# Attention output transposed by DMA planes instead of TensorE, in a linear-attention and soft-tree layer

## What is computed

```python
xn = layernorm(x)
Q, K = elu(xn @ Wq + bq) + 1, elu(xn @ Wk + bk) + 1   # 16 heads of 64
V = xn @ Wv + bv
KV_t = KV_{t-1} + k_t v_t^T ; Ks_t = Ks_{t-1} + k_t   # causal, per head
attn = (q_t KV_t) / (q_t . Ks_t + 1e-6)               # 16 heads side by side: 1024 features
tree = leaf_probs(sigmoid(xn @ Wt.T @ routers.T)) @ leaf_values @ Wout.T + bout   # 256 leaves
out = x + attn @ Wo + bo + tree
```

## Time and profile before

| | us |
|---|---|
| median of 3 runs | 1233.66 |
| range of the runs | 1233.03 to 1235.53 |
| the profiled execution, its own time | 1235.54 |
| its span, first to last instruction | 1233.8 |

### The profile page before, as it was taken

How to read it: one execution, slowest core, us unless ns; L and a number is a source line. 1 busy time by engine, 2 the same in 40 slices (tenths; PEclk the granted TensorE clock), 3 DMA queues, 4 the chain that set the end, 5 groups by cost and what they waited for, 6 DMA issues and landing times.

```text
span 1233.8 us, 48282 instructions
## 1 busy us (share of the span) xinstructions
PE 1202.1 (97%) x21669; PEld 1052.3 (85%) x21669; DVE 811.4 (66%) x2186; ACT 551.7 (45%) x881; POOL 675.5 (55%) x842
## 2 busy tenths in 40 slices
PE   5899999999999999999999999999999999999987
PEld 4789889898988989889898988989889898988967
DVE  4774876757667574875758667574866758667462
ACT  3553552535445253552535445253552535445251
POOL 3475556455554665556455554655556465554550
PEclk9999999999999999999999999999999999999998
DMA  6121211212123121222213122121222213122120
GB/s 230 20 53 36 57 34 45 54 36 54 36 46 53 37 54 36 57 34 45 54 36 54 36 46 53 36 54 36 55 36 45 53 36 54 36 45 36 37 36 19
DMA packets 154654, 58.94 MB, mean 48 GB/s; under 512 B 134081, under 2 KB 152784, under 8 KB 154448
## 3 DMA queue, kind: packets, MB, share of 16 engines
q1 hardware_dynamic: 154448, 55.86, 21.8%
HBM read 14.43 MB, written 8.39 MB: 18 GB/s over the span
## 4 chain that ended last, share of the span: by engine, by line
PE 95%; DVE 2%; ACT 1%; POOL 1%; DMA 1%; issue 1%; SPq 0%; POOLq 0%; DVEq 0%
PE s_pair L705 26%; PE w_pair L705 22%; PE o_pair L717 9%; PE s_pair L717 9%; PE o_pair L814 6%; PE s_pair L778 5%; PE o_pair L828 5%; PE kv_pair L789 5%; PE w_pair L758 5%; PE w_pair L740 2%; DMA ffn_tok<-in_L_ffn_Wout_w_dram 1%; ACT ex L455 0%; ACT ex L458 0%; PE o_pair L705 0%; DVE wk L250 0%
## 5 line engine op out<-in xcount | busy, mean ns | idle before, releaser
L353 POOL TENSOR_SCALAR_AFFINE_SELECT aT<-aT 64x512 f32<-64x512 f32 x256 | 167.7, 655 | 366.0 <-ACT aT L482 357.1
L482 ACT ACTIVATE aT<-s_pair 128x512 f32<-128x512 f32 x128 | 76.4, 597 | 337.6 <-PE s_pair L778 337.6
L705 PE MATMUL w_pair<-xnT,wk 128*128 128x512 f32 x768 | 212.3, 412 | 4.1 <-ACT k_tok L468 2.2
L705 PE MATMUL s_pair<-xnT,wq 128*128 128x512 f32 x756 | 200.9, 401 | 1.4 <-POOL aT L353 1.1
L632 DVE TENSOR_TENSOR snaps<-kv_pair,snaps 128x65 f32<-128x65 f32 x768 | 173.3, 226 | 26.5
L404 POOL COPY k_tok<-k_turned 128x1024 uint16<-128x1024 uint16 x126 | 171.4, 1361 | 29.6 <-POOL aT L353 22.6
L396 POOL COPY k_planes<-kT 128x1024 uint16<-128x1024 uint16 x126 | 131.2, 1041 | 95.1 <-POOL k_tok L404 58.2
L455 ACT ACTIVATE ex<-w_pair,neg_bias 128x512 f32<-128x512 f32 x130 | 89.6, 689 | 189.5 <-PE w_pair L705 189.5
L705 PE MATMUL s_pair<-wv,xnT 128*128 128x512 f32 x648 | 168.5, 394 | 0.1
L458 ACT ACTIVATE ex<-ex 128x512 f32<-128x512 f32 x256 | 161.9, 633 | 8.1
L705 PEld LDWEIGHTS w_pair<-xnT,wk 128*128 128x128 f32 x768 | 134.4, 188 | 36.2 <-ACT k_tok L468 2.7
(11 more groups left out here) (107 smaller groups left out, 1972.1 us busy)
## 6 DMA issues: line engine op xcount, KB each, us to landing
x_in<-in_L_attn_x_dram SPq DMA_DIRECT2D x16, 512.0 KB, 5.1
out_dram<-y_buf SPq DMA_DIRECT2D x32, 256.0 KB, 2.1
k_turned<-k_planes SPq DMA_TRANSPOSE x126, 3.1
stage<-in_L_attn_Wv_dram SPq DMA_DIRECT2D x2, 512.0 KB, 8.0
stage<-in_L_attn_Wk_dram SPq DMA_DIRECT2D x2, 512.0 KB, 9.6
stage<-in_L_attn_Wq_dram SPq DMA_DIRECT2D x2, 512.0 KB, 10.9
stage<-in_L_attn_Wo_dram SPq DMA_DIRECT2D x2, 512.0 KB, 9.4
bv_all<-in_L_attn_bv_dram SPq DMA_DIRECT2D x1, 512.0 KB, 8.6
```

The lines of the kernel that those rows point to most:

```text
L353: pool.affine_select(out=part, in_=part, compare_op=ALU.is_ge, fill=0.0, base=0, pattern=[[0, 2 * CH], [1, D]], channel_multiplier=-1).the ...
L482: act.activation(aT[:, n % 2].rearrange("p h c q -> p h (c q)"), s_pair[:, :, 0:CH * D], ACT.Copy).then_inc(s_copied, 1)
L705: last = pe.matmul(dst, l, r, start=i == 0, stop=i == len(steps) - 1)
```

## The change

For the units n >= 3 with p < 7 (`by_dma`, 109 of 128) the oT fill and what read it are gone. Their outputs are turned as the keys are: POOL copies the 16-bit halves of `o_tok` into two planes (`take_output_apart`, behind the mask), SP issues a transposing DMA ahead of that of the keys, and in the next unit ACT interleaves the two turned planes into a float32 tile (`put_output_together`, a 128 x 1024 copy of 16-bit elements in SBUF, behind the exponential of K and ahead of the head's work). ACT takes the high part from that tile behind the exponential of Q (`high_of_turned`), DVE the low part at the end of the unit (`low_of_turned`, both inputs in SBUF); at p = 7 both stand ahead of the high and low part of the remaining oT.

The head now fills bank S1 and the tail W1. DVE does `norm(n)` ahead of `carry(n+1)`. PE's waits stand elsewhere: at single matmuls, for the values at the outer products, for each output bank at its first use, and y waits for the low parts of tile t = 0 and t = 6 (`o_low`). Odd tiles of a block are kept with their halves swapped; for this each load of x is three DMAs instead of one, and each half store of a block three instead of one. The number of matmuls for everything else is the same.

```diff
+def by_dma(n):
+    return n % PAIRS < PAIRS - 1 and n >= 3
@@ unit_fills
-    fills += [(name, W1) for name in head]
+    fills += [(name, S1) for name in head]
...
-    fills += [(name, S1) for name in tail]
-    fills.append((("oT", p, g), W1))
+    fills += [(name, W1) for name in tail]
     if p == PAIRS - 1:
-        fills += [(("y", 0, g), O1), (("y", 1, g), S1)]
+        fills += [(("oT", p, g), W1), (("y", 0, g), O1), (("y", 1, g), S1)]
+    elif not by_dma(n):
+        fills.append((("oT", p, g), S1))
@@ SP
+            def load_block(g):
+                dst, src, done = x_in[:, g % 2], x_rows[g], x_loaded[g % 2]
+                sp.dma_start(dst[:, 0::2], src[:, 0::2]).then_inc(done, 16)
+                sp.dma_start(dst[0:D, 1::2], src[D:P, 1::2]).then_inc(done, 16)
+                sp.dma_start(dst[D:P, 1::2], src[0:D, 1::2]).then_inc(done, 16)
+            def turn_output(n):
+                g, p = divmod(n, PAIRS)
+                sp.wait_ge(o_apart, units_by_dma(n))
...
+                if n >= 5:
+                    sp.wait_ge(o_whole, units_by_dma(n) - 2)
+                sp.dma_start_transpose(o_turned(p), o_planes.rearrange("p s n -> p (s n)")).then_inc(o_turned_in, 16)
@@ POOL, in a unit
                 if n + 1 < UNITS:
                     mask(n + 1)
+                if by_dma(n):
+                    take_output_apart(n)
                 if n + 2 < UNITS:
                     put_together(n + 2)
@@ ACT
+            def put_output_together(n):
+                g, p = divmod(n, PAIRS)
+                k = units_by_dma(n)
+                act.wait_ge(o_turned_in, 16 * k)
+                act.activation(o_full[:, 1, p].bitcast(U16).rearrange("p (n s) -> p s n", s=2),
+                               o_turned(p).rearrange("p (s k) q -> p s (k q)", s=2), ACT.Copy).then_inc(o_whole, 1)
+            def high_of_turned(n):
+                g, p = divmod(n, PAIRS)
+                act.wait_ge(o_whole, units_by_dma(n))
+                act.activation(oT[:, 0, p], o_full[:, 1, p], ACT.Copy).then_inc(oT_hi, 1)
...
                     if kind in "KQ":
                         exponential(name)
+                        if kind == "K" and turned:
+                            put_output_together(n - 1)
+                        if kind == "Q" and turned:
+                            high_of_turned(n - 1)
+                            turned = False
@@ DVE
+            def low_of_turned(n):
+                g, p = divmod(n, PAIRS)
+                dve.wait_ge(oT_hi, n + 1)
+                dve.tensor_tensor(oT[:, 1, p], o_full[:, 1, p], oT[:, 0, p].bitcast(F32), ALU.subtract)\
+                   .then_inc(o_low, 1)
...
+                norm(n)
                 if n + 1 < UNITS:
                     carry(n + 1)
-                norm(n)
@@ PE
+                        if c == 0 and t in (0, PAIRS - 2):
+                            until(o_low, units_by_dma(g * PAIRS + max(t, PAIRS - 3)))
```

More of the change, by code:

```diff
@@ L25, with units_by_dma @@
 W0, W1, S0, S1, O0, O1 = range(6)
+def by_dma(n):
+    return n % PAIRS < PAIRS - 1 and n >= 3
+def units_by_dma(n):
+    return sum(by_dma(m) for m in range(n + 1))
 def unit_fills(g, p, blocks):
@@ L155, in attention_and_tree_layer, with o_turned @@
         k_turned = sb("k_turned", [P, 2 * CH, P], U16)
+        o_planes = leaf_odd.rearrange("p c n -> p (c n)").bitcast(U16).rearrange("p (s n) -> p s n", s=2)
+        def o_turned(p):
+            place = gate if p < HALF else xn
+            return place[:, 2 * (p % 2):2 * (p % 2) + 2].rearrange("p c n -> p (c n)").bitcast(U16)\
+                .rearrange("p (k f) -> p k f", f=P)
         aT = sb("aT", [P, 2, 2, CH, D])
@@ L164, in attention_and_tree_layer @@
         with nc.sbuf_tensor("stage", [P, 4, KT_ * inner], F32) as stage:
+            pass
+        with nc.sbuf_tensor("o_full", [P, 2, PAIRS, TOK], F32) as o_full:
             pass
@@ L239, in attention_and_tree_layer @@
         o_normed = sem("o_normed")
+        o_apart = sem("o_apart")
+        o_turned_in = sem("o_turned_in")
+        o_whole = sem("o_whole")
+        o_low = sem("o_low")
         oT_hi = sem("oT_hi")
@@ L672, in _ @@
                 fills = [name for name, _ in unit_fills(g, p, BLOCKS)]
+                turned = n and by_dma(n - 1)
                 for name in values_first(fills, p):
@@ L739, in fill @@
                     for c in range(CH):
-                        last = pe.transpose(dst[:, c * P:(c + 1) * P], src[:, c, i * P:(i + 1) * P], ident[:, :])
+                        to = dst[:, c * P:(c + 1) * P].rearrange("p (a q) -> p a q", a=2)
+                        to = to[:, ::-1] if c % 2 else to
+                        last = pe.transpose(to, src[:, c, i * P:(i + 1) * P], ident[:, :])
                 elif kind == "gate":
@@ L935, in _, with normed, head_ready @@
                 fills = unit_fills(n // PAIRS, n % PAIRS, BLOCKS)
-                first_by_vector = any(bank == W1 and name[0] in ("V1", "xT", "leaf") for name, bank in fills)
+                def normed():
+                    until(o_normed, n + 1)
+                def head_ready():
+                    for kind, i, g in (f for f, _ in fills):
+                        if kind == "xT":
+                            until(xn_ready, g + 1)
+                        if kind == "leaf" and i == 0:
+                            until(leaf_step, (g + 1) * LEVEL_STEPS)
                 def masked():
@@ L957, in _ @@
                             until_drained(("xT", t, g))
-                    if kind == "leaf" and i == 0:
+                    if kind == "leaf":
                         until(leaf_step, (g + 1) * LEVEL_STEPS)
@@ L962, in _ @@
                             until_drained(("leaf", t, g))
-                    fill(name, masked if kind == "Q" else whole if bank == S1 and kind != "y" else None)
+                    fill(name, head_ready if kind == "K" else normed if kind == "Q" else masked if bank == W1 and kind in ("V0", "V1") else None)
                     if kind == "y" and i == 0:
-                        whole()
+                        masked()
+                normed()
                 masked()
-                whole()
 _INS = ['L0_attn_x', 'L0_attn_Wq', 'L0_attn_bq', 'L0_attn_Wk', 'L0_attn_bk', 'L0_attn_Wv', 'L0_attn_bv',
```

78 lines of the change are left out of this document (53 added, 25 removed).

## The result

The changed kernel takes 1276.93 us, median of 4 runs (1275.27 to 1278.43), against 1233.91 of before: 1.0348 times as long, 95% interval 1.0329 to 1.0366. Its profiled span is 1276.7 us, 42.9 more; 35.2 were forecast.

What follows compares the result with a forecast made beforehand. PE, 95% of the chain, sets the time but its scores wait for queries through ACT; 14 inner blocks x 2.28 = 31.9, plus first block 0.9, last 0.7, start 0.8, end 0.9: +35.2, 1269 us, range 1232 to 1300.

Steps and rivals of the forecast that it cites:

- rival C: The interleaving write is dear on ACT too, delay 1.24 us: 1295 us; chance 0.13, cases between included.
- What leaves PE: Four transposes per fill take 0.53 us of PE; 109 fills give 57.8 us if nothing else binds.
- p = 1, 3, 4: In these units the queries come 0.95 us later through ACT's copy, against slack 0.42: +0.53 us each.
- p = 2: DVE takes the values first, so phi of Q already stands 0.62 us behind what ACT allows: +0.33 us.
- p = 5: ACT already waits 0.79 us for PE's fill of Q; the queries stay and their slack is gained: -0.42 us.
- p = 6: ACT waits for PE's fill here too, but the values ahead of phi leave no slack: 0.
- p = 7: At y PE waits 0.9 us for tile 6's low part and 0.3 more for the remaining tile's: +1.2 us.
- p = 0: No copy in this unit, and the same slack as p = 5: -0.42 us.
- What costs nothing: POOL's extra 1041 ns per unit, SP's DMAs and DVE's norm ahead of carry stay hidden; keys have 1.7 us cover.
- A: Gain in full, since the queries are not what PE meets next: 1178 us; chance 0.16, partial gain included.
- B: ACT's copy at its lower bound, 0.54 us: a block +0.2 us, 1238 us; chance 0.06.
- D: PE's standing lowers its clock: far above 1400 us if for the whole run; chance 0.03, other waits above 1300 included.

Runs made afterwards that it cites:

- copy_ahead_of_keys: The changed kernel with ACT's copy moved ahead of the exponential of K, behind the copy of the scores; 1219.76 us, 0.9894 of before.
- norm_first_before: The kernel before with DVE's norm put ahead of the running sums, no other edit; 1233.0 us, 1.0012 of before.
- x_behind_queries: The changed kernel with DVE normalising the next block's x at p = 0 behind phi of Q; 1268.02 us, 1.0293 of before.
- carry_first: The changed kernel with DVE's running sums put ahead of norm again, all else as changed; 1291.28 us, 1.047 of before.
- low_later: copy_ahead_of_keys with the low part from the end of p = 1 taken in p = 2 behind norm and sums; 1216.96 us, 0.9876 of before.

## Why the prediction was right, and where it was not

Direction, mechanism and place were right: PE's scores wait for the queries, which wait for ACT's copy; in 1276.9 against 1269 the error is 8 us. That it is so small is in part luck. The copy delays ACT by 1.23 us and not by 0.95, and with 1.24 the prediction's own sum gives 1295 (rival C); several smaller errors of the other sign, below, took most of that back.

**What leaves PE**, 0.53 us a fill: confirmed by 7.38 - 6.83 = 0.55 where nothing else binds.

**p = 1, 3, 4**, +0.53: measured +0.54, but by errors that cancel. The copy delays ACT by 547.85 - 546.62 = 1.23 us, not 0.95; it was the upper bound that was true. Against it, the head's work now delays Relu of Q by 548.32 - 547.85 = 0.47, not 0.58. In the earlier trace rows Relu of Q also waited for its fill, though no wait is marked: the fill ended at 526.96 + 1.64 = 528.60, Relu began at 528.64. So 0.11 more was free. The fill in the kernel before, timeline:

```profile
526.96 1.64 PE L705 MATMUL s_pair<-xnT,wq 128*128 128x512 f32 x6
```

PE starts its scores 550.50 - 550.44 = 0.06 behind phi, not 0.15, so the slack was 0.51. 1.23 - 0.11 - 0.51 = 0.61, and 0.06 of it is given back behind the scores: Relu of K follows their start by 545.36 - 542.57 = 2.79 us, before by 526.80 - 523.95 = 2.85.

**p = 2**, +0.33: +0.47. The Exp of Q comes 1.08 us later behind the scores (6.47, before 5.39), less the 0.62 of the prediction. PE also stands there 0.5 us at the outer products, for the values, which follow the low part of xT and so the copy. **p = 5**, -0.42, and **p = 6**, 0: -0.39 and -0.02. At p = 5 two errors cancel again: Relu of Q does come later (5.73 us behind the scores, before 5.67), and the slack was 0.51, which leaves 0.45; the block shown gained 0.46. Without the copy in the chain p = 5 takes 7.77, so the copy costs 0.15 there and not nothing.

**p = 7**, +1.2: +1.22. The waiting and the places were as said (changed kernel):

```profile
574.12 0.68 DVE L698 TENSOR_TENSOR oT<-o_full,oT 128x512 fp32r<-128x512 f32 x1
...
574.72 0.68 DVE L684 TENSOR_TENSOR oT<-w_pair,oT 128x512 fp32r<-128x512 f32 x1
...
574.86 1.23 PE L827 MATMUL o_pair<-wo,oT 128*128 128x256 f32 x6 [0.69 <-DVE oT L698]
...
575.93 0.86 PE L827 MATMUL o_pair<-tree_w,leafT 128*128 128x256 f32 x6
```

The 18 matmuls ahead of tile 6 began at 571.91, so at 0.117 us each PE was there at 574.01 and stood 0.85 us (0.69 is marked). The last six took 575.93 - 574.86 = 1.07 us instead of 0.70, 0.37 more, behind the remaining tile's low part. Forecast were 0.9 and 0.3. Here too errors cancel: the copy is 0.28 us longer in its effect, and the low part took 0.68 us, not 0.9.

In copy_ahead_of_keys, in a block where one of POOL's gate instructions had begun just before it, it took 1.55 us.

**p = 0**, -0.42: +0.14, the step that failed. I took over the slack of p = 5 and let DVE's order cost nothing ("ahead of the next `from_state`"), without adding up what stands ahead of phi of Q at p = 0: norm, sums, normalising, phi of K and values. In place of the 7.91 us forecast p = 0 took 8.47, held by that row and not by ACT or PE; the order of norm and sums alone made p = 0 only 0.1 longer in the kernel before (norm_first_before). 0.56 us in 14 inner blocks is 7.8 us. With the 0.14 of p = 2, 2.0 us in 14 blocks, that is all by which the inner blocks exceed the forecast, 41.5 against 31.9; the first and last block, start and end took 1.4 us instead of 3.3. x_behind_queries, with the normalising out of that row, took 1268.0, against the 1269 forecast; its p = 0, 7.80, is PE's own bound, 0.11 below the 7.91 forecast.

**What costs nothing**: true in the changed kernel: PE waited for the keys 2.1 us in the whole span. But POOL's addition of x and bias at p = 1 (2.4 us) was left out of the cover. With units of 7.9 us this stayed hidden at p = 2; in units of 6.8 us, 1.1 shorter, PE waited for the keys there.

**Rivals.** A, the full gain, was not to be had: with the copy elsewhere and three more edits the best kernel gained 32 us of 56. B is out, C was right in the copy's length and wrong in its price (I had added it to an unchanged slack). D is out: the granted clock was 1.00, full speed, in a unit in which PE stood 0.86 us. The changed kernel by stretches: span; busy PE, PEld, DVE, ACT, POOL; granted clock; DMA share; GB/s.

```profile
543.30:551.20 7.90, 7.04 (x164) 5.71 (x156) 6.04 (x17) 5.35 (x8) 4.76 (x5) 1.00 0.55 70
```

## What to carry to other kernels

An engine at 95% of the chain does not give back what is taken off it if a wait a few tenths of a us away belongs to another engine; measure that slack before moving work, and put the moved work into a wait of its new engine, not between two links of a chain. Here the same copy, moved ahead of two instructions of ACT, turned 3.5% slower into 1.1% faster. A slack in one kind of unit does not carry over to the next: add up each engine's row of work ahead of each hand-over, by unit.

## What the runs showed of the hardware

In these kernels a DVE subtraction with both inputs in SBUF that met a POOL instruction reading SBUF ended a fixed time behind the end of that POOL instruction. Alone the low part takes 0.68 us. It ended 0.55 us behind POOL's addition in copy_ahead_of_keys; in carry_first, 531.71 + 1.84 = 533.55 against POOL's end at 533.00, also 0.55. Of the 109 low parts of the changed kernel 15 took more than 0.85 us, and all of these ended 0.54 to 0.56 us behind POOL's addition, which had begun before them; in low_later it is 19, 0.53 to 0.55 us behind a copy or a gate instruction of POOL. It goes the other way round too: the POOL copy that began at 578.09 in low_later, within the low part, took 1.37 us instead of 1.04. This is no sharing at half speed. The Trainium skill, SBUF — State Buffer, section "SBUF: two separate sides", calls the pair of ports that the two share an exclusive lock which the first to start holds for its whole instruction, for a DVE instruction with two SBUF inputs against a POOL instruction that reads SBUF; the traces agree with these ends. The normalising has one input that is a tile, and yet four of its instructions took 1.38 us at the start, beside no POOL copy, 2.27 beside one (before) and 3.17 beside two (carry_first); how the two hold each other there was not tested.

ACT's copy of 1024 16-bit elements took 1041 ns with its writes side by side and 1362 ns with them 4 bytes apart (the first also read one plane twice). The Trainium skill, ScalarE: Activation LUTs, section "Step-by-step: what each stage is for", gives one element per cycle and lane, for 1024 elements an estimate of 0.85 us plus a start-up; this fits the first and not the second. A row with the same writing pattern, on POOL (1361 against 1041 ns), was the better guide.
